# Opening of a two-layer kernel: later x groups loaded behind the second group's, the first values loaded from ScalarE's queue

## What is computed

```python
ifg = jnp.concatenate([q, k, v], axis=-1)          # q = layernorm(x), k = v = ctx
ig = (ifg @ igate_w.T + igate_b).T
fg = (ifg @ fgate_w.T + fgate_b).T
...
log_f = jax.nn.log_sigmoid(fg)
cs = jnp.cumsum(log_f, axis=1)
...
max_log_D = jnp.max(log_D, axis=-1, keepdims=True)
D_mat = jnp.exp(log_D - max_log_D)
C = qk * D_mat
normalizer = jnp.maximum(jnp.abs(C.sum(axis=-1, keepdims=True)), jnp.exp(-max_log_D))
h = jnp.einsum('hst,htd->hsd', C / (normalizer + EPS), vh)
```

## Time and profile before

| what | value |
|---|---|
| median of the runs | 586.76 us |
| the profiled execution's own time | 586.5 us |
| its span, first to last instruction | 584.9 us |
| PE busy | 548.8 us, 94% of the span |
| DVE, ACT, POOL busy | 330.9, 230.3, 80.1 us |
| mean granted TensorE clock | 0.993 |

### The profile page before, as it was taken

The page is one execution under the profiler, slowest core; times in us unless marked ns, Lnnn a source line. Parts: engine busy times, 40 slices in busy tenths (PEclk is TensorE's granted clock), DMA queues, the critical chain, the costliest instruction groups (busy, mean ns, idle before and its releaser), DMA issues.

```text
span 584.9 us, 8490 instructions
## 1 busy us (share of the span) xinstructions
PE 548.8 (94%) x2765; PEld 446.0 (76%) x2773; DVE 330.9 (57%) x802; ACT 230.3 (39%) x436; POOL 80.1 (14%) x121
## 2 busy tenths in 40 slices
PE   6698988999999998899999999999999999999993
PEld 5476665688888877678888878888788888788883
DVE  6569889778777588663353453443543534633331
ACT  2244645547788644362122251122441122621120
POOL 5223324202311233100000100000000001000001
PEclk9999999999999999999999999999999999999998
DMA  7675628344958797200000000000000000000001
GB/s 198 161 167 169 143 79 194 115 162 140 391 190 234 208 322 147 81 1 0 1 0 1 36 2 1 0 1 9 28 0 1 1 1 37 0 1 0 1 0 38
DMA packets 57760, 47.69 MB, mean 82 GB/s; under 512 B 37278, under 2 KB 48542, under 8 KB 57316
## 3 DMA queue, kind: packets, MB, share of 16 engines
q1 hardware_dynamic: 51960, 28.29, 18.7%
q0 software_dynamic: 5616, 18.88, 9.7%
q10 hardware_dynamic: 148, 0.04, 0.0%
HBM read 40.58 MB, written 2.10 MB: 73 GB/s over the span
## 4 chain that ended last, share of the span: by engine, by line
PE 67%; DVE 4%; ACT 2%; issue 1%; POOL 0%; DVEq 0%; ACTq 0%; POOLq 0%
PE ps L896 54%; PE ps L588 4%; PE ps L589 4%; PE ps L574 1%; DVE xn L1248 1%; PE ps L843 1%; PE ps L580 1%; PE ps L584 1%; PE ps L581 1%; ACT al L1175 1%; ACT h L1211 0%; DVE sc L1493 0%; DVE x L1518 0%; DVE x L1460 0%; ACT kr L1162 0%
## 5 line engine op out<-in xcount | busy, mean ns | idle before, releaser
L896 PE MATMUL ps<-hBt,h 128*128 128x512 f32 x512 | 117.9, 390 | 0.1
L896 PE MATMUL ps<-hA,h 128*128 128x512 f32 x512 | 117.3, 390 | 0.0
L1211 ACT ACTIVATE h<-ps,scol 128x512 f32<-128x512 f32 x64 | 44.2, 690 | 175.4 <-PE ps L896 175.3
L896 PEld LDWEIGHTS ps<-hBt,h 128*128 128x128 f32 x512 | 95.7, 188 | 20.8 <-DVE hBt L1539 1.1
L896 PEld LDWEIGHTS ps<-hA,h 128*128 128x128 f32 x512 | 95.9, 188 | 20.4 <-DVE hA L1539 0.6
L896 PE MATMUL ps<-xT,w 128*128 128x512 f32 x256 | 61.9, 396 | 1.8 <-DVE h L1534 1.1
L896 PEld LDWEIGHTS ps<-xT,w 128*128 128x128 f32 x256 | 46.2, 188 | 15.9 <-issue 6.6
L1557 DVE CAST hBt<-h 128x512 fp32r<-128x512 f32 x32 | 13.7, 427 | 73.7 <-ACT h L1211 73.7
L1557 DVE CAST hA<-h 128x512 fp32r<-128x512 f32 x32 | 13.7, 427 | 70.0 <-ACT h L1211 70.0
L431 POOL TENSOR_TENSOR rstd<-ve,mhalf 128x4 f32<-128x4 f32 x16 | 16.7, 1046 | 207.9 <-DVE ve L1243 207.9
L1194 ACT ACTIVATE silD<-ps,scol 128x512 f32<-128x512 f32 x32 | 22.0, 688 | 47.5 <-PE ps L896 47.5
(11 more groups left out here) (175 smaller groups left out, 895.8 us busy)
## 6 DMA issues: line engine op xcount, KB each, us to landing
looked<-w_all_in SPq DMA_DIRECT2D x16, 704.0 KB, 5.6
h<-w_all_in POOLq DMA_DIRECT2D x16, 512.0 KB, 6.5
V<-ctx_in SPq DMA_DIRECT2D x32, 128.0 KB, 4.4
Qb<-xT SPq DMA_DIRECT2D x64, 64.0 KB, 2.1
w<-w_all_in POOLq DMA_DIRECT2D x3, 1024.0 KB, 7.0
x<-x_in SPq DMA_DIRECT2D x4, 512.0 KB, 4.9
kstA<-ctxT_in SPq DMA_DIRECT2D x4, 512.0 KB, 5.4
kstC<-ctxT_in SPq DMA_DIRECT2D x4, 512.0 KB, 5.7
```

The source lines that it names most:

```text
L896: last = mm(o, a, b, start=(k == 0 and p == 0), stop=(k == n_k - 1 and p == 1))
L1211: fn(h32[:, m % 2, :], ps[:, 2 + m % 4, :], ACT.Gelu, scale=scol[:, L + 1, m:m + 1])\
```

## The change

Three things are moved; nothing is computed otherwise. The loads of `x` for groups three and four go from behind the first queries to right behind the second group's `x`. The four loads of the first `V` go from SP to ACT, ahead of ACT's first work and behind the same two semaphore counts of `const_set`. The issue of `gi` on SP is now in front of the waits for `const_set` and `qb0_set`, with no `V` load ahead of it.

```diff
@@ -275,6 +275,9 @@
                 sp.dma_start(Lr[0:3, u, :, :, :], ones_rows_in[0:3, 0]).then_inc(s["consts"], 16)
             sp.dma_start(tri[:, :, :], tri_in).then_inc(s["consts"], 16)
             sp.dma_start(x[:, Q:2 * Q, :], x_in[Q:2 * Q].rearrange("b s d -> s b d")).then_inc(s["x_second"], 16)
+            for g in range(2, G):
+                sp.dma_start(x[:, Q * g:Q * g + Q, :], x_in[Q * g:Q * g + Q].rearrange("b s d -> s b d"))\
+                    .then_inc(s["x_rest"], 16)
             sp.dma_start(lns[:, :], lns_in.partition_broadcast(P)).then_inc(s["consts"], 16)
@@ -312,15 +315,11 @@
+            sp.wait_ge(s["gate_copied"], 1)
+            sp.dma_start(gi[:, :], gsb[0:NH, :].rearrange("h (q t) -> h q t", q=Q)).then_inc(s["gate_moved"], 16)
             sp.wait_ge(s["const_set"], 2)
             sp.wait_ge(s["qb0_set"], 1)
-            values(0, 0)
-            sp.wait_ge(s["gate_copied"], 1)
-            sp.dma_start(gi[:, :], gsb[0:NH, :].rearrange("h (q t) -> h q t", q=Q)).then_inc(s["gate_moved"], 16)
             queries_in(0, 0, 0)
-            for g in range(2, G):
-                sp.dma_start(x[:, Q * g:Q * g + Q, :], x_in[Q * g:Q * g + Q].rearrange("b s d -> s b d"))\
-                    .then_inc(s["x_rest"], 16)
@@ -1057,6 +1056,10 @@
             table_set(EXP_AND_LN)
+            act.wait_ge(s["const_set"], 2)
+            for q in range(Q):
+                act.dma_start(V[:, 0, q, 0:NH, 0:DH], ctx_in[q].rearrange("t (h d) -> t h d", d=DH))\
+                    .then_inc(v_ld[0], 16)
             k_hi(1, kstA[:, :, :], 0)
             x_hi(0, 0)
             gate_copy(0, QK)
```

## The result

| | before | changed |
|---|---|---|
| median of 6 runs each, us | 586.82 (585.94 to 588.28) | 593.35 (590.59 to 594.7) |
| ratio, 95% interval | | 1.010 (1.0073 to 1.0127) |
| the profiled execution, us | 586.5 | 591.6 |
| its span, us; mean granted clock | 584.9; 0.993 | 589.9; 0.99 |
| PE starts its loop (L619, now L618) at, us | 26.75 | 33.27 |

The changed kernel is slower by 6.5 us between the medians, and by 1.0% in the ratio, which is not the ratio of the medians. The direction is as predicted; the size is not: 588.4 was forecast, with 590.3 as the upper end.

The account below looks back on a forecast made before the run. The start of PE's loop, waiting for the row copies behind the gate chain, was taken to carry any shift to the end. 586.5 + 1.6 - 0.2 = 587.9, plus 0.26 for the median and 0.2 for the clock: 588.4 us, range 586.3 to 590.3.

Parts of the forecast that it names:

- The loop's start decides: PE's loop start at L619, 26.75 us: any shift of it should pass to the end one for one.
- ACT is held by its four issues: ACT's V issues ahead of kstA: 5.6 us (2.2 to 6.4), so kstA 3.1 us late; chance 0.42.
- The allowance for a slow first issue: ACT's V issues: 0.6 us added to the far end because ACT's own first issue, of gf, took 1.33 us.
- The way from `gsb` to `fmn`: Gate copy's end at 17.9 to fmn: gi lands 2.3 us after its issue, fmn at about 20.2, +1.6 us.
- The DMA engines' own end: Loads ahead of gi: 16.4 us of transfer, through at 18.4 to 18.9, fmn 0.9 to 1.4 us late.
- this rival: Opening: ACT's issues quick, 2.2 to 3 us, DMA work delays gi; +0.2 to +1.0 us in all; chance 0.13.
- The clock: PE's granted clock: a fall in the gates +1.2 to 2.4 us, the later fall gone -1.2; entered as +0.2.
- The rival that named the fall: PE's gates: the clock falls there too, 1.2 to 2 us more, 589.2 to 590.6 us; chance 0.23.
- The row copies: Copies ahead of the loop: without x beside them they gain 0 to 1.3 us, taken as 0.2.
- The consts, the second `kstA`, `V` and the early `x` for their readers: Opening loads: they land later or are issued later, but still before their readers need them; no cost.
- its fourth rival: SP and ACT: ACT done by 8.69, gi leaves at 14.8, -0.93 us, 584.8 to 585.9 us; chance 0.09.

Follow-up runs that it names:

- e8: Changed kernel with V's four loads on ACT behind gf and the early x behind the load of diag: 586.16 us, ratio 1.0002.
- e6: Changed kernel with all four V loads on ACT moved behind the issue of gf: 587.60 us, ratio 1.0018.
- e2: Kernel before with only V moved to ACT, gi first on SP and x left behind the queries: 594.81 us, ratio 1.0133.
- e10: e6 with four extra 128 KB loads, in 128 pieces of 1 KB each, ahead of ACT's first work: 586.74 us, ratio 1.0005.
- e4: Changed kernel with two V loads ahead of ACT's first work and two behind the issue of gf: 586.43 us, ratio 0.9976.
- e9: Changed kernel with 33 matmuls that nobody reads in PE's idle time before the gates: 592.26 us, ratio 1.0096.
- e1: Kernel before with only the x loads of groups three and four moved early; V and gi stay on SP: 588.69 us, ratio 1.0023.
- e7: Kernel before, all on SP, with x behind the load of diag, then gi, V, queries and row copies: 586.40 us, ratio 1.0001.
- e11: e7 with 14 instead of 8 repeated matmuls ahead of the loop: 585.85 us, ratio 0.9993.
- e3: Kernel before with gi issued ahead of V, all still on SP: 590.96 us, ratio 1.0075.

## Why the prediction was wrong in size

**The loop's start decides: right.** From the first matmul with the feed-forward weights (at 118.6 to 128.5 us) to the end it took 464.2 to 465.3 us in all fourteen profiled executions. The loop over groups in front of it varies more, by the falls of the clock in it: 92.2 to 92.4 us where there is none (e8, the changed kernel), 93.1 before, and 96.2 at most (e6). So the loop's start carries the 6.5 us, but a gain of 1 to 2 us there can drown in the falls behind it.

**ACT is held by its four issues: right in kind, and the failed step in size.** For these four issues the forecast took 5.6 us, with 6.4 as the far end, from the later loads of `V` beside POOL's queue. Measured were 9.86, and 7.12 without the early `x` (e2). It was the wrong neighbour: in the earlier trace rows SP issues `V` while one other queue moves large pieces at 67.4%. Here SP's queue alone fills the engines, and for 3.4 us leaves ACT's almost nothing (8 of 814 pieces). The term was +3.1 us at `kT` and measured +7.42, 4.3 more, against a miss of 4.95 us between forecast and measured median. The allowance for a slow first issue was wrong as well: the first took 694 ns, and the third and the fourth were the slow ones.

**The way from `gsb` to `fmn`: right.** 2.3 us were forecast from the end of the gate copy, plus a little; measured were 2.59 instead of 3.79 before. The 0.93 us of SP's wait are in it. The releaser is now `gf` on ACT's queue, with an issue of 1.60 us. DVE waits 2.12 us for it rather than under 0.5: the norm's end moved by 7.2 us and `gsb` by 8.9, so 1.7 of the wait come from there.

**The DMA engines' own end: hidden here, and borne out elsewhere.** As a second bound the forecast had the engines through at 18.4 to 18.9 and `fmn` at 19.5 to 20.0, 0.9 to 1.4 us late even with quick issues. In the changed kernel ACT's hold put `fmn` at 26.30, far behind it, so the kernel itself says nothing of it. e10 does: there the issues are quick, `x` and 512 KB more are in front of the gate rows, and `fmn` is at 19.46, 0.9 us late. With half of `V` in front it is at 18.12 (e4), with none of it at 17.77 (e6). So the sum of 16.4 us was about right. It did not decide, for the quick issues that this rival assumed didn't come.

**The clock: both signs came.** The forecast weighed +1.2 to 2.4 in the gates against -1.2 behind the loop's start and entered +0.2. The table shows +1.49 in the gates, and e9 prices the fall at 1.3. Behind the loop's start, the way to the next gates became 1.4 shorter in the profiled execution. In sum they nearly cancel there: 5.1 us between the two profiled executions (591.6 and 586.5) against 6.5 at the loop's start. The medians lie 6.5 apart. The likely reason is that other executions of the changed kernel have falls in the loop too: four of its other five have a mean granted clock of 0.983 to 0.987, against 0.990 in the profiled one. No trace of them shows where. The rival that named the fall had the mechanism and not the price, because it stood on the same 5.6 us.

**The row copies: mis-sized.** Taken were 0.2 with 1.3 as the far end; measured 1.20, from `zp` to the loop 2.39 instead of 3.59. e1 shows the same 2.39 and e2, with `x` back in its old place, 3.83. So `x` did slow them, even though the engines' share had fallen before the third copy moved. The row that argued for 0.2 is a mean over all 16 engines, and doesn't tell when the last piece of a copy lands.

**The consts, the second `kstA`, `V` and the early `x` for their readers: free, as said.** In the changed kernel no wait for them shows in DVE's or ACT's timeline up to the loop.

**Issue early, wait late:** the rule that the forecast took from the Trainium skill's "DMA: Bandwidth & Descriptors" (Rules for kernel authors) for its fourth rival, holds for the engine that issues the loads of e10 (2.02 us of issue, and `kT` waits for its own load). It leaves out what they do to others: the gate rows came 1.7 us later than in e6. It fails for `V` in 128-byte pieces, where issuing is itself the wait.

**What stays open.** Why ACT's queue got 8 pieces of 814 between 7.5 and 10.9 us wasn't isolated (it got 332 of 1073 in e2 and 100 of 972 in e9). Nor is it shown what ends a long issue. The forecast's reading, that it stands until earlier pieces have drained, fits, but with no fixed number: 590 pieces of `V` had moved when the third issue of the changed kernel ended, 2775 when the fourth did, and 1786 at the end of the third in e2. Whether one of the better orders (e4, e7, e11) beats the kernel before isn't settled: their loops start 1.1 to 2.0 us sooner, but all the intervals contain 1.

## What to carry to other kernels

A load in many small pieces can hold the engine that issues it for a time that its own size doesn't tell: here it went with how many pieces of the same queue stood before it and with what the other queue still had to move. Two such loads in front of ACT's work cost nothing (1.41 us, e4), four cost 9.86. So put such issues behind the engine's first critical work or in front of it only as far as they are free. The same bytes in pieces eight times as long held ACT for a fifth of the time, but still delayed the small copies behind them. When a bound is priced from another place in the same kernel, ask whether the neighbouring queue there moves as much and gives way as readily. And taking one wait from a serial queue moves it to what stands last in that queue (e3), so move the traffic and the order together (e7).

## What the runs showed of the hardware

- Two queues on the same DMA engines moved 992 and 949 pieces in the same 3.1 us: about one for one, not byte for byte. The queue with pieces of 128 bytes got an eighth of the other's bytes.
- The issue of a load with 1024 pieces took 0.68 to 5.23 us in one and the same group of four; with 128 pieces, 0.41 to 0.60. The first two of a group on ACT took 0.58 to 0.90 us each in every kernel, also beside SP's large loads.
- Falls of PE's granted clock in the loop differ from execution to execution of nearly the same code, and the times of one kernel go with the mean clock: in 25 runs of the kernel before on one chip, the nine at 0.992 or more took 583.79 to 587.11 us and the eight at 0.986 or less took 587.50 to 592.98. The first two rows are stretches of e1 with a fall, and the one below them is e8's whole loop without any:

```profile
51.00:56.00 5.00, 4.99 (x20) 3.61 (x20) 2.36 (x4) 2.44 (x5) 3.11 (x3) 0.66 0.18 44
79.00:83.00 4.00, 4.00 (x17) 3.31 (x17) 2.19 (x3) 1.65 (x3) 2.90 (x2) 0.57 0.19 49
```

```profile
27.00:122.00 95.00, 85.77 (x475) 61.86 (x482) 77.32 (x231) 49.51 (x124) 29.86 (x52) 1.00 0.55 138
```

The falls seen lasted 3.4 or 6.8 us. The span less the loop's start was 556.6 with none behind it (the changed kernel and e8), and 558.2 to 559.1 with one of 3.4 us (five kernels). With two it was 560.2 in e2 and e9 but 558.0 in e4. In the other four a fall had begun ahead of the loop's start, and reached into it: 560.3 in e1, 559.5 in e3, 560.9 in e6 and 560.7 in e10. So one fall of 3.4 us costs 0.7 to 2.5 us. What sets them off in one execution and not in another isn't shown.
